# Count matrix of a graph kernel: three short one-hots by one VectorE comparison, and a table entry loaded at another place

## The reference, cut to what matters

```python
dst = jnp.minimum((2500 * uniform((40000,)) ** 2.0).astype(int32), 19999)
order = jnp.argsort(dst, stable=True)        # the edges come sorted by destination
src, dst = src[order], dst[order]            # src: uniform in 0..2499
...
out = segment_sum(alpha[:, :, None] * h[src], dst, num_segments=N)   # attention
agg = segment_sum(x[src], dst, num_segments=N)                       # mean aggregation
```

## Time and profile before

| what | us |
|---|---|
| median of 3 runs | 2090.7 |
| lowest, highest | 2088.82, 2093.08 |
| the profiled execution | 2094.36 |
| its span in the profile | 2092.5 |
| the one-hots for C, first to last start | 37.2 to 298.5 |

### The profile page before, as it was taken

The page is one execution under the profiler, slowest core; times in us unless marked ns, Lnnn a source line. Parts: engine busy times, 40 slices in busy tenths (PEclk is TensorE's granted clock), DMA queues, the critical chain, the costliest instruction groups (busy, mean ns, idle before and its releaser), DMA issues. The chain is left out here.

```text
span 2092.5 us, 62466 instructions
## 1 busy us (share of the span) xinstructions
PE 1699.5 (81%) x21608; PEld 1342.3 (64%) x21608; DVE 1559.0 (75%) x3518; ACT 1345.5 (64%) x2207; POOL 283.4 (14%) x446
## 2 busy tenths in 40 slices
PE   3988874889989739998992699998989985588883
PEld 1222223888988528898891577775549984588883
DVE  6999988899999889999997522222332257899986
ACT  0256546999999569999994522221113364899986
POOL 2555510566600000000000000000000000000000
PEclk8999997899999869999995999999999997799997
DMA  2100000001010000101101200000010010000002
GB/s 75 15 2 2 2 1 27 28 28 40 28 40 28 1 30 28 40 28 39 39 17 55 93 2 0 0 0 8 0 36 23 20 59 14 12 23 21 21 21 100
DMA packets 34806, 54.83 MB, mean 26 GB/s; under 512 B 10708, under 2 KB 26256, under 8 KB 34448
## 3 DMA queue, kind: packets, MB, share of 16 engines
q1 hardware_dynamic: 30992, 51.59, 7.5%
q0 software_dynamic: 3584, 0.06, 0.1%
HBM read 43.14 MB, written 8.49 MB: 25 GB/s over the span
## 5 line engine op out<-in xcount | busy, mean ns | idle before, releaser
L1104 ACT ACTIVATE Rm<-rows,cB 128x1280 bf16<-128x1280 f32 (+3 forms) x816 | 847.2, 1132 | 32.8 <-DVE Mn L1139 19.6
L1241 PE MATMUL ps<-R,M 128*128 128x132 f16 (+1 forms) x8640 | 685.2, 221 | 116.9 <-DVE Mn L1139 62.9
L1241 PEld LDWEIGHTS ps<-R,M 128*128 128x128 f16 x8640 | 546.2, 97 | 140.7 <-DVE M L1149 51.0
L1149 DVE TENSOR_TENSOR M<-Rm,C 128x1280 f16<-128x1280 bf16 (+3 forms) x816 | 527.5, 672 | 37.5 <-ACT Rm L1104 26.9
L1234 PE MATMUL ps<-HB,C 128*128 128x66 f16 x6400 | 304.7, 194 | 60.5 <-DVEq L1130 60.5
L1234 PEld LDWEIGHTS ps<-HB,C 128*128 128x128 f16 x6400 | 259.6, 98 | 60.7 <-DVEq L1130 60.7
L640 PE MATMUL acc<-ohc,ohl 128*128 128x500 f16 x806 | 217.9, 382 | 43.1 <-DVE ohl L597 35.3
L1152 DVE SCALAR_TENSOR_TENSOR M<-rows,cN,C 128x1280 f16<-128x1280 f32 (+1 forms) x144 | 217.0, 1507 | 0.0
L595 DVE TENSOR_SCALAR ohc<-cells,near 128x1000 f16<-128x1000 f16 x403 | 195.7, 486 | 23.6 <-PE acc L640 18.1
L640 PEld LDWEIGHTS acc<-ohc,ohl 128*128 128x128 f16 x806 | 52.5, 98 | 200.9 <-DVE ohl L597 177.3
L431 POOL DMA_INDIRECT wd<-wv,wi x112 | 139.6, 1247 | 150.8 <-issue 110.7
(11 more groups left out here) (296 smaller groups left out, 2265.9 us busy)
## 6 DMA issues: line engine op xcount, KB each, us to landing
rows<-rowd SPq DMA_DIRECT2D x32, 640.0 KB, 3.9
rows<-rowd SPq DMA_DIRECT2D x16, 320.0 KB, 3.4
xd<-R SPq DMA_DIRECT2D x4, 640.0 KB, 2.9
xr<-xd SPq DMA_DIRECT2D x20, 128.0 KB, 2.0
xd<-HB SPq DMA_DIRECT2D x1, 2560.0 KB
xr<-xd SPq DMA_DIRECT2D x5, 512.0 KB, 6.5
R<-in_x SPq DMA_DIRECT2D x1, 2432.0 KB
xr<-in_x SPq DMA_DIRECT2D x19, 128.0 KB, 2.0
```

The lines of the kernel that those rows point to most:

```text
L1104: a.activation(Rm[:, s % SG, 0:wide(p)], rows[:, p % 2, 0:wide(p)], ACT.Relu, bias=cB[:, ds(h + s * nh, 1)]).then_inc(s_R, 1)
L1149: v.tensor_tensor(M[:, u, 0:wide(p)], Rm[:, u, 0:wide(p)], Cs, ALU.min).then_inc(s_M if s in ONE else s_cut, 1)
L1241: m = pe.matmul(region(p % 2, r), lhsT, rhs, start=split and opens and r % 3 == 0, stop=True, skip_group_check=True)
```

## The change

The 128-wide one-hots of several chunks are made by one `tensor_tensor` comparison instead of one `tensor_scalar` each: one for the two chunks ahead, and one for the three chunks of a turn. Its first operand is `lows`, the row 0..127 three times; its second is `low16`, an f16 copy of `bT` made once in the set-up, each value read 128 times (`to_broadcast`). `ohl` now has three groups of three: group 0 for the chunks ahead, groups 1 and 2 by turns. The group is written before the first `ohc` of a turn, with a wait of its own for the same count of `s_used`. `s_oh` counts one per group and one per `ohc`. TensorE takes its weights from an address in a register. The next range's entry is loaded behind the first `ohc` of a range instead of ahead of it. `tmp` and `zero` of the set-up move into `HB`.

```diff
-        lows = sb("lows", [P, P], f16, edge)
+        LANES = 3
+        lows = sb("lows", [P, LANES * P], f16, edge)
+        low16 = sb("low16", [P, NG * P], f16, edge)
...
-            tmp = ph.sb("tmp", [P, NG * P], f32)
-            zero = ph.sb("zero", [P, 512], f32)
+            tmp = HB[:, 3 * NG * P:4 * NG * P]
+            zero = HB[:, 4 * NG * P:4 * NG * P + 512]
...
-                g.iota(lows[:, :], pattern=[[1, P]], base=0, channel_multiplier=0,
+                g.iota(lows[:, :], pattern=[[0, LANES], [1, P]], base=0, channel_multiplier=0,
...
+                ch(v.tensor_copy(low16[:, :], bT[:, :]))
...
-            ohl = ph.sb("ohl", [P, U3, P], f16)
+            ohl = ph.sb("ohl", [P, 3 * LANES * P], f16)
...
+            def lows_of(group, lanes):
+
+                return ohl[:, ds(group * (LANES * P), LANES * P)].rearrange("p (u j) -> p u j", u=LANES)[:, 0:lanes, :]
+
+            def low_of(group, u):
+
+                return ohl[:, ds(group * (LANES * P), LANES * P)].rearrange("p (u j) -> p u j", u=LANES)[:, u, :]
+
+            def group_of(turn):
+
+                return 1 + nc.s_assert_within(turn % 2, 0, 1, skip_runtime_bounds_check_because="a remainder")
...
-                    if q + 1 < NW:
-                        coming = packed(v, q + 1)
                     v.wait_ge(s_near, q // NEAR + 1)
                     own = cells[:, q % NEAR * CELLS:(q % NEAR + 1) * CELLS]
+
+                    def lows_group(k, group, lanes):
+                        v.tensor_tensor(lows_of(group, lanes), lows[:, :].rearrange("p (u j) -> p u j", u=LANES)[:, 0:lanes, :],
+                                        low16[:, ds(k, lanes)].unsqueeze(2).to_broadcast([P, lanes, P]),
+                                        ALU.is_equal).then_inc(s_oh, 1)
 
                     def one(i, u):
                         k, w = chunk(first + i * U3 + u, NG * P - 1), slot_of(q, u)
                         v.wait_ge(s_used, (before + i) * U3 + (q * AHEAD + u + 1))
                         v.tensor_scalar(ohc[:, w, :], own, near[:, q // NEAR % 2, ds(k, 1)], None,
                                         ALU.is_equal).then_inc(s_oh, 1)
-                        v.tensor_scalar(ohl[:, w, :], lows[:, :], bT[:, ds(k, 1)], None,
-                                        ALU.is_equal).then_inc(s_oh, 1)
-
+
+                    v.wait_ge(s_used, before * U3 + (q * AHEAD + 1))
+                    lows_group(chunk(first, NG * P - LANES), 0, AHEAD)
                     for u in range(AHEAD):
                         one(0, u)
+                        if u == 0 and q + 1 < NW:
+                            coming = packed(v, q + 1)
                     with v.Fori(0, threes) as i:
+                        v.wait_ge(s_used, (before + i) * U3 + (q * AHEAD + AHEAD + 1))
+                        lows_group(chunk(first + i * U3 + AHEAD, NG * P - LANES), group_of(before + i), U3)
                         for u in range(AHEAD, AHEAD + U3):
                             one(i, u)
...
-                        pe.wait_ge(s_oh, (before + i) * (2 * U3) + ((q * AHEAD + u) * 2 + 2))
+                        group, lane = (0, u) if u < AHEAD else (group_of(before + i), u - AHEAD)
+                        made = q * (AHEAD + 1) + (u + 2 if u < AHEAD else u + 3)
+                        pe.wait_ge(s_oh, (before + i) * (U3 + 1) + made)
...
-                            ins = pe.matmul(bank(b, q % 2), ohl[:, w, :], ohc[:, w, d0 * NT:d1 * NT],
+                            ins = pe.matmul(bank(b, q % 2), low_of(group, lane), ohc[:, w, d0 * NT:d1 * NT],
```

## The result

| what | before | after |
|---|---|---|
| median, us | 2091.5 (4 runs) | 2107.9 (4 runs) |
| lowest, highest | 2088.8, 2093.1 | 2105.4, 2109.3 |
| ratio, 95% interval | | 1.0079 (1.0067 to 1.0091) |
| the profiled execution, its span | 2094.4, 2092.5 | 2109.3, 2107.5 |

The changed kernel is 16 us slower. The forecast was 2 to 3 us slower with a range up to 2103, so the time lies outside it. The loss arises in the stage that builds C: its last ScalarE copy of a range starts at 300.23 us before and at 317.15 after, 16.9 us later, where the spans of the two profiled executions differ by 15.0. The counts of chunks, turns and matmuls are the same.

A forecast was written before the change was run, and what follows sets the result against it. VectorE was taken to bound the stage that builds C. Terms of +6.7 us by kind of range, -4 for stretches and +0.5 set-up gave +3.2 us: 2093.9 against the median, range 2082 to 2103.

The forecast's parts named there:

- The set-up: Before the C stage: 256 more values of `lows` on GpSimd and the f16 copy on VectorE, +0.5 us together.
- The rival without a closed chain: C stage: way back 0.6 us, turn stays 1.65, range ends gain 0.36; -10 us, 2081; chance 0.05.
- that with two values a cycle: C stage: the group's comparison runs at two values a cycle; -8 to -15 us, 2079; chance 0.12.
- the sum of the chain: From one group to the next: 1.87 us against 1.65, +0.22 a turn; +6.2 us over 28 later turns.
- the 0.77 of the way back: From a chunk's first weight load on TensorE to VectorE's next instruction waiting for the freed slot: 0.77 us.
- TensorE's wait on a register instruction: New chain step ahead of a turn's first matmul: some 0.05 us, bounds 0 and 0.1.
- VectorE's register instructions between wait and group: New chain step on VectorE: one more register instruction, 0.06 us, bounds 0 and 0.1.
- the stretches: One-hots stretched beside GpSimd, hidden where a turn now waits for TensorE: -4 us, from 0 to -6.
- The range ends: Moved entry load, hidden beside an `ohc`: -0.2 us in each of 6 ranges without search or product, -1.2 us.
- the exposed load: Case that the entry load is not hidden behind the `ohc`: up to +5 us; chance 0.11 shared with the longer chain.
- the slower rival: C stage: new steps 0.1 each, way back 0.85, turn 2.04; +12 us, 2103; chance 0.11 shared with load not hidden.

## Why the prediction missed

**What held.** VectorE bounded the stage before; the comparison runs at one value a cycle (0.56 us; forecast 0.55 against 0.35); as VectorE work the grouping is worth nothing (0.47 + 3 x 0.39 = 1.64 us a turn); the turn becomes a chain from group over `ohc`, weight load and used slot to the next group, with TensorE and VectorE waiting for each other. The set-up cost 0.6 us (forecast 0.5). The rival without a closed chain, and that with two values a cycle, fell.

**The step that failed is the sum of the chain**, 1.87 us forecast, 2.06 measured in range 0 and 2.16 in the ranges behind it. Its group, `ohc` and the 0.77 of the way back were right. Two new terms were mis-sized:
- TensorE's wait on a register instruction: 0.05 us forecast with a bound of 0.1, 0.14 measured (0.20 with it, 0.06 without, with everything else the same).
- VectorE's register instructions between wait and group: 0.06 forecast with a bound of 0.1; measured 0.15 in range 0 (0.92 less the 0.77 of the earlier trace rows) and 0.25 elsewhere (1.02 less 0.77). The number of instructions was right: one in the 0.77, as ahead of an `ohc`, and one more. Their length was not. I had taken 57 ns for each; they take 0.13 and 0.07 us in range 0, 0.22 and 0.08 elsewhere. The fixed read gave back 0.10 us a turn in range 0 and 0.19 in range 1.

I had priced each by the length of a register instruction of another place. The bounds, 0 and 0.1, came from that too and were not bounds: the instructions ahead of a group and ahead of a turn's first matmul are longer than those in the rows, and a wait on one adds the 0.05 us on either side of it. With the turns as measured, 13 beyond the second in range 0 and 15 in ranges 1 to 8 give 13 x 0.41 + 15 x 0.51 = +13.0 us in place of +6.2.

By kind of range, without the set-up, the forecast before its 4 us for the stretches are taken off:

| ranges | forecast | measured |
|---|---|---|
| range 0 | +3.0 | +5.2 |
| 8 ranges of 3 to 6 turns | +4.0 | +7.4 |
| 14 ranges of 2 turns | +1.3 | +2.7 |
| 5 ranges of 1 turn, with a search | +0.8 | -0.3 |
| ranges 28 to 49 | -2.3 | +1.3 |
| sum | +6.7 | +16.3 |

**The range ends.** For the 6 ranges without search or product the forecast was 0.2 us less each, 2.92; they take 3.29 (0.06 more than before). From the first `ohc` of a turn into the next of these ranges, changed kernel:

```profile
258.53 1.25 DVE L613 TENSOR_SCALAR ohc<-cells,near 128x1000 f16<-128x1000 f16 x3
...
259.20 0.11 PEld L664 LDWEIGHTS acc<-ohc,ohl 128*128 x2 [0.99 <-issue]
...
259.99 0.42 DVE L606 TENSOR_TENSOR ohl<-lows,low 128x256 f16<-128x256 f16 x1 [0.21 <-PE acc L664]
```

From `ohc` to load it is 0.67 in place of 0.58, TensorE's step again. The way back to the pair is 0.79, near the 0.77 taken. The rest is between the pair and the turn's group: 259.99 to 261.35 is 1.36 us, where 1.11 was forecast. "It lies beside an `ohc` and costs nothing" was wrong: the load alone is 0.32 and the `ohc` holds VectorE 0.39, but the queue has its other register work to do in that time, and the turn's group comes 0.2 later for it. I had named the exposed load as part of the slower rival, with up to 5 us; taking it back gives 3.4.

**What was given back** (4 us for the stretches beside GpSimd) can't be told apart in the sum. The stretches did go: `ohc` fell by 11 ns in the mean, 403 x 0.011 = 4.4 us of VectorE's work. But the measured column above already holds whatever reached the end, and in range 0 and the eight after it (+12.6) it is about what the longer turns give by themselves (+13.0). So little of the 4 us is to be seen there. No run took GpSimd away.

The slower rival, both steps at 0.1 and the way back at 0.85, had the right mechanism and 2103; I gave it and the exposed load 0.11 together. That its turn of 2.04 is close to the 2.06 of range 0 is in part luck: the way back without the new step is 0.77 and not 0.85, and the new steps are larger than 0.1. The range ended where its assumed bounds did.

## What to carry to other kernels

A merged instruction inherits the strictest wait of its parts; ask for each buffer what it needs, since waiting one count too long can put the merged work into the loop between two engines. Where such a loop is nearly closed, register instructions between a wait and the instruction that it releases are on the path: price them by rows of the same kind of instruction, or give them wide bounds, and read a turn in more than one range: here the first range is 0.1 us a turn faster than all others. For an f16 comparison with a value read over and over, hold each value twice and let the innermost axis step over the two: that kept the fast rate here.

## What the runs showed of the hardware

- A two-operand f16 comparison of 384 elements takes 0.56 us with one element repeated innermost and 0.36 us with a pair repeated. The Trainium skill says so for the first case ("Vector Engine (DVE) Microarchitecture Reference", section 5.1, Performance modes: one element read 16 times over ran at one a cycle, and a row read again and again at two), and these runs agree for 128 reads.
- From the end of `ohc` to the weight load it is 0.20 us where the wait stands on a register instruction (weights at an address in a register), and 0.06 us where it stands on the matmul itself (weights at a fixed address).
- Register instructions under one name in the profile differ by a factor of four: 57 ns in the median for an `ohc`'s address, 65 to 243 ns for a group's. The same two instructions of the group's line take 0.13 and 0.07 us in the first range, 0.22 and 0.08 in the others.
- Reading the second operand of 151 comparisons at a fixed address takes one register instruction away ahead of each, shortens the turn by 0.10 to 0.19 us, and is worth 14 us of 2108 here.
